# Opening stage of a gated cross-attention kernel: keys and values of its tiles in two PSUM banks by turns, other slots for the latents and weights

## The reference, cut to what matters

```python
lat = layer_norm(layernorm(x), ln_lat_g, ln_lat_b)      # x: (4, 512, 256)
ctx = layer_norm(ctx_1024, ln_ctx_g, ln_ctx_b)          # (4, 1024, 256)
q = (lat @ Wq)                                          # 16 heads of 64
k, v = split(ctx @ Wkv, 2)
k = apply_rope(k, cos, sin)                             # k*cos + swapped halves*(-sin, sin)
attn = softmax(clip(q @ k.T / 8, -11, 11)) @ v
x = x + tanh(g_xattn) * (attn @ Wo + bo)
x = x + tanh(g_ffn) * moe_ffn(layernorm(x))             # 4 experts, top 2, exact gelu
```

## Time and profile before

| | |
|---|---|
| time of three runs, median (lowest to highest) | 1143.57 us (1140.17 to 1144.3) |
| the profiled execution: its own time | 1138.58 us |
| its span (first to last instruction) | 1137.0 us |
| mean granted TensorE clock | 0.985 of full |
| TensorE busy | 1078.4 us, 95% of the span |
| VectorE / ScalarE / GpSimd busy | 951.9 / 653.4 / 536.8 us |
| the stage ahead of the attention, up to the first scores | 46.62 us |

### The profile page before, as it was taken

One profiled execution on the slowest core, in us unless ns is written; L12 is line 12 of the kernel. 1 busy time (PEld: TensorE's weight loads), 2 busy tenths in 40 slices (PEclk: granted clock), 3 DMA queues, 4 the chain that ended last, 5 costly groups with the idle time before them and its releaser, 6 DMA issues.

```text
span 1137.0 us, 22328 instructions
## 1 busy us (share of the span) xinstructions
PE 1078.4 (95%) x7949; PEld 718.2 (63%) x7949; DVE 951.9 (84%) x1772; ACT 653.4 (57%) x1259; POOL 536.8 (47%) x551
## 2 busy tenths in 40 slices
PE   5799999999999999999999999999999998899995
PEld 4455555656565555556555555655445998899994
DVE  6698899898989989898999989879976757777675
ACT  4555557655555765454566655544556666577662
POOL 6433376333427634342654334417641655656661
PEclk9999999999999999999999999989999999899998
DMA  6100000000000000000000000601264342565344
GB/s 167 52 10 11 19 25 24 15 12 13 10 20 21 28 11 11 19 11 20 19 29 10 11 10 10 201 1 39 71 202 141 120 141 85 171 193 181 113 143 146
DMA packets 59188, 72.04 MB, mean 63 GB/s; under 512 B 11580, under 2 KB 52168, under 8 KB 59081
## 3 DMA queue, kind: packets, MB, share of 16 engines
q1 hardware_dynamic: 54840, 61.30, 17.5%
q0 software_dynamic: 3360, 8.53, 2.0%
q10 hardware_dynamic: 880, 0.79, 0.2%
HBM read 54.84 MB, written 16.54 MB: 63 GB/s over the span
## 4 chain that ended last, share of the span: by engine, by line
PE 74%; DVE 13%; issue 4%; POOL 3%; ACT 2%; DMA 2%; SPq 0%; DVEq 0%; POOLq 0%
PE pv L1808 17%; PE sc L1794 14%; PE kv L1739 5%; PE kv L1741 5%; PE kv L1740 5%; PE sc L1739 4%; PE sc L1740 4%; PE sc L1741 4%; PE tr L1780 3%; PE mi L1739 2%; PE mi L1818 2%; PE mi L1740 2%; PE mi L1741 2%; DVE acc L1167 2%; DVE prob L1152 2%
## 5 line engine op out<-in xcount | busy, mean ns | idle before, releaser
L926 ACT ACTIVATE prob<-sc 128x1024 f32<-128x1024 f32 x256 | 249.4, 1029 | 203.4 <-PE sc L1794 200.8
L711 POOL TENSOR_TENSOR rot_s<-k_raw,sinb 128x256 f32<-128x256 f32 x128 | 110.8, 866 | 383.9 <-ACT k_raw L871 383.8
L1808 PE MATMUL pv<-prob,val 128*32 128x512 f32 x2048 | 247.9, 602 | 3.0 <-DVE recip L1186 3.0
L1152 DVE TENSOR_SCALAR prob<-prob 128x1024 f32<-128x1024 f32 x256 | 181.3, 721 | 48.1 <-ACT prob L926 47.0
L1794 PE MATMUL sc<-q_hid,w2all 64*128 64x512 f32 x1536 | 214.1, 411 | 0.0
L1794 PEld LDWEIGHTS sc<-q_hid,w2all 64*128 64x128 f32 x1536 | 135.7, 186 | 100.4 <-issue 56.2
L1167 DVE TENSOR_TENSOR acc<-acc,prob 128x1024 f32<-128x1024 f32 x120 | 178.2, 1505 | 0.0
L715 POOL TENSOR_TENSOR rot_c<-rot_c,rot_s 128x256 f32<-128x256 f32 x128 | 111.8, 874 | 41.6 <-DVE rot_c L1141 27.0
L1808 PEld LDWEIGHTS pv<-prob,val 128*32 128x32 f32 x2048 | 56.9, 110 | 113.4 <-issue 92.1
L1739 PE MATMUL kv<-w2all,acts 128*128 128x512 f32 x256 | 115.2, 450 | 6.6 <-DVE rot_c L1141 5.3
L1741 PE MATMUL kv<-w2all,acts 128*128 128x512 f32 x256 | 103.5, 404 | 0.0
(11 more groups left out here) (306 smaller groups left out, 2372.8 us busy)
## 6 DMA issues: line engine op xcount, KB each, us to landing
prob<-in_L_ffn_w SPq DMA_DIRECT2D x17, 1024.0 KB, 5.4
slots_x<-lat_r SPq DMA_DIRECT2D x1, 5016.0 KB, 18.7
rows<-slots_x SPq DMA_DIRECT2D x19, 264.0 KB, 5.0
rows<-in_ctx SPq DMA_DIRECT2D x32, 128.0 KB, 2.1
w_raw<-in_L_xattn_Wq SPq DMA_DIRECT2D x16, 256.0 KB, 2.8
w_raw<-in_L_xattn_Wo SPq DMA_DIRECT2D x64, 64.0 KB
acc<-in_L_ffn_w SPq DMA_DIRECT2D x16, 256.0 KB, 5.1
acc<-in_L_ffn_w SPq DMA_DIRECT2D x5, 512.0 KB, 5.2
```

The lines of the kernel that those rows point to most:

```text
L711: g.tensor_tensor(rot_s[:].rearrange("p (h a c) -> p h a c", h=4, a=2), kh[:, :, ::-1, :], sinb[:, t].unsqueeze(1).to_broadcast([P, 4, 2, ...
L926: a.activation(prob[:, s % 2, i, :], sc[i][:], ACT.Exp, scale=DH ** -0.5).then_inc(exp_done[i], 1)
L1152: v.tensor_scalar(prob[:, s % 2, i, :], prob[:, s % 2, i, :], EXP_LOW, EXP_HIGH, ALU.max, ALU.min).then_inc(clamped[i], 1)
L1808: last = mm(pv[g * 32:(g + 1) * 32, :], val[:, u % 2, 2 * c + i, at:at + 32], prob[:, s % 2, i, h * N:(h + 1) * N], start=c == 0 and i == ...
```

## The change

The `before()` lists get another order on four engines, and two of the waits change:

- `kv_bank`: in the first unit the tiles with an odd number have their keys and values in the bank `pv`, which nothing else uses before the attention's second step. `kv_make` of tile i then waits for `rot_cos` of tile i-2 and not i-1. `kv_evac` and `rot_cos` read the bank in question. In all other units everything stays in `kv`.
- `kv_evac` waits for `rot2` (the first of GpSimd's two instructions of `rotate`) and no longer for `rot`; in exchange GpSimd itself waits for its own last `rot` ahead of the product. This holds for all units.
- VectorE: `lat_stats` stands in slot 3 (was 2), `lat_norm` in slot 5 (was 4, behind the rotation), `q_low` in slot 9 (was 8), all of them and `wkv_low` now ahead of `rot_cos` and `k_low` of their slot; `wkv_low` of units 1 to 3 in slots 6, 8, 10 (was 4, 6, 8).
- ScalarE: `wq_round` in slot 3 (was 4), `q_round` in slot 8 (was 7), `wkv_round` in slots 3, 4, 7 (was 3, 5, 7).
- GpSimd: `lat_scale` and `wq_low` ahead of `rotate` in their slots, `lat_scale` in slot 4 (was 3).
- TensorE: `ctx_turn` ahead of `k_turn`; `q_make` in slot 8 (was 7).

```diff
+        def kv_bank(b, u, t):
+
+            return pv if is_first(b, u) and t % 2 else kv
+
...
@@ rotate
                 pool.wait_ge(kraw_out, n + 1)
+                wait(pool, rot, n)
                 g.tensor_tensor(rot_s[:].rearrange("p (h a c) -> p h a c", h=4, a=2), kh[:, :, ::-1, :],
...
@@ gpsimd, before
-                    if 0 <= t - 3 < ST:
-                        rotate(0, 0, t - 3)
-                    if t == 3:
+                    if t == 4:
                         lat_scale(0)
                     if t == 5:
                         wq_low(0, 0)
+                    if 0 <= t - 3 < ST:
+                        rotate(0, 0, t - 3)
...
@@ kv_evac
-                wait(act, rot, kv_no(b, u, t))
-                a.activation(k_raw[:], kv[:, 0:UW], ACT.Copy).then_inc(kraw_out, 1)
-                a.activation(val[:, u % 2, t, :], kv[:, UW:2 * UW], ACT.Copy).then_inc(kv_out, 1)
+                wait(act, rot2, kv_no(b, u, t))
+                bank = kv_bank(b, u, t)
+                a.activation(k_raw[:], bank[:, 0:UW], ACT.Copy).then_inc(kraw_out, 1)
+                a.activation(val[:, u % 2, t, :], bank[:, UW:2 * UW], ACT.Copy).then_inc(kv_out, 1)
...
@@ scalar, before
-                    if t == 4:
+                    if t == 3:
                         wq_round(0, 0)
                     if t in (5, 6):
                         lat_affine(0, t - 5, sc[1][:, (t - 5) * N:(t - 4) * N])
-                    if t == 7:
+                    if t == 8:
                         q_round(0, 0)
-                    if t in (3, 5, 7):
-                        wkv_round(t // 2)
+                    if t in (3, 4, 7):
+                        wkv_round((3, 4, 7).index(t) + 1)
...
@@ vector, before
-                    if t == 2:
-                        wkv_low(0)
+                    if t in (2, 6, 8, 10):
+                        wkv_low((2, 6, 8, 10).index(t))
                     if 0 <= t - 2 < ST:
                         ctx_split(t - 2)
...
                         dve.wait_ge(const, 6)
+                    if t == 3:
                         for i in range(NT):
                             lat_stats(0, i)
                             dve.wait_ge(l_st, i + 1)
                             lat_aggregate(0, i)
+                    if t == 5:
+                        for i in range(NT):
+                            lat_norm(0, i)
+                    if t in (6, 7):
+                        lat_low(0, t - 6)
+                    if t == 9:
+                        q_low(0, 0)
                     if 0 <= t - 3 < ST:
                         rot_cos(0, 0, t - 3)
                     if 0 <= t - 4 < ST - 1:
                         k_low(0, 0, t - 4)
-                    if t == 4:
-                        for i in range(NT):
-                            lat_norm(0, i)
-                    if t in (6, 7):
-                        lat_low(0, t - 6)
-                    if t == 8:
-                        q_low(0, 0)
-                    if t in (4, 6, 8):
-                        wkv_low((t - 2) // 2)
...
@@ kv_make
-                wait(pe, rot1, kv_no(b, u, t))
+                wait(pe, rot1, t - 1 if is_first(b, u) else kv_no(b, u, t))
...
@@ tensor, before
                         kv_make(0, 0, t - 3)
+                    if 0 <= t - 1 < ST:
+
+                        wait(pe, c_affd, t - 2)
+                        ctx_turn(0, t - 1, sc[0][:, ((t - 1) % 2) * N:((t - 1) % 2 + 1) * N])
                     if 0 <= t - 4 < ST - 1:
                         k_turn(0, 0, t - 4)
-                    if 0 <= t - 1 < ST:
-
-                        wait(pe, c_affd, t - 2)
-                        ctx_turn(0, t - 1, sc[0][:, ((t - 1) % 2) * N:((t - 1) % 2 + 1) * N])
                     if t in (5, 6):
                         lat_turn(0, t - 5, sc[1][:, (t - 5) * N:(t - 4) * N])
-                    if t == 7:
+                    if t == 8:
                         q_make(0, 0)
```

More of the change, by code:

```diff
@@ L1140, in rot_cos @@
                 dve.wait_ge(kv_out, kv_no(b, u, t) + 1)
-                v.tensor_tensor(rot_c[:].rearrange("p (h c) -> p h c", h=8), kv[:, 0:UW].rearrange("p (h c) -> p h c", h=8),
+                v.tensor_tensor(rot_c[:].rearrange("p (h c) -> p h c", h=8),
+                                kv_bank(b, u, t)[:, 0:UW].rearrange("p (h c) -> p h c", h=8),
                                 cosb[:, t].unsqueeze(1).to_broadcast([P, 8, HALF]),
@@ L1767, in kv_make @@
                 pe.wait_ge(c_ready, tile_no(b, t) + 1)
-                wait(pe, rot1, kv_no(b, u, t))
+                wait(pe, rot1, t - 1 if is_first(b, u) else kv_no(b, u, t))
                 for k in range(KT):
-                    last = three(kv[:].rearrange("p (w n) -> p w n", w=2), lambda l: ctx_t[:, l, k, t * P:(t + 1) * P],
+                    last = three(kv_bank(b, u, t)[:].rearrange("p (w n) -> p w n", w=2), lambda l: ctx_t[:, l, k, t * P:(t + 1) * P],
                                  lambda l: wkv[:, l, k, :].rearrange("p (w n) -> p w n", w=2)[:, :, u * UW:(u + 1) * UW],
@@ L1905, in before @@
                         kv_make(0, 0, t - 3)
-                    if 0 <= t - 4 < ST - 1:
-                        k_turn(0, 0, t - 4)
                     if 0 <= t - 1 < ST:
@@ L1911, in before @@
                         ctx_turn(0, t - 1, sc[0][:, ((t - 1) % 2) * N:((t - 1) % 2 + 1) * N])
+                    if 0 <= t - 4 < ST - 1:
+                        k_turn(0, 0, t - 4)
                     if t in (5, 6):
                         lat_turn(0, t - 5, sc[1][:, (t - 5) * N:(t - 4) * N])
-                    if t == 7:
+                    if t == 8:
                         q_make(0, 0)
```

## The result

| | before | changed |
|---|---|---|
| median (lowest to highest) of 7 runs each | 1142.26 us (1140.17 to 1144.3) | 1133.73 us (1129.95 to 1135.23) |
| profiled execution, its span | 1138.58, 1137.0 us | 1131.16, 1129.6 us |
| first scores | 46.62 us | 39.01 us |
| third step's scores | 57.51 us | 49.58 us |
| span behind the first scores | 1090.4 us | 1090.6 us |

A forecast was written before the change was run, and what follows sets the result against it. No engine is full before the first scores; their start decides. 18.9 + 18.4 + 0.8 + 1.6 = 39.7 against 46.62 gives 6.9, less 0.5 for the clock 6.4, from the median 1143.57: 1137.0 us, range 1133 to 1142.

The forecast's parts named there:

- Part 1: VectorE, slots 2 and 3: latents' statistics behind tile 3 cover the 1.11 us wait for x; tile 0's rot_cos at 13.3.
- Part 2: GpSimd's latent chain decides when VectorE gets its next work: lat_norm can start at 18.9 us, where it was 19.52.
- Part 3: VectorE from lat_norm to the last wkv_low has no idle time: 18.4 us of work plus 0.8 of new waits.
- These two are the bank's and `k_raw`'s: VectorE's waits of 1.17 and 2.63 us for a tile's values, counted as removed by the two banks: 3.8 us.
- The rival that "the turn of the banks doesn't free anything": Both value waits come back under another name, only Parts 1 and 2 gain, 1 to 2.5 us: 1141.5 us; chance 0.12.
- The new list's own waits: VectorE after lat_norm: tile 7's split waits for ScalarE, which waits for tile 6's split; with small ones 0.8 us.
- Part 4: VectorE and GpSimd slowing each other in the stage: some 3.4 us of old overlaps held in 18.4, plus 1.6 new.
- The rival that pays each in full: All ten or so overlaps block VectorE for a whole add, 7.4 us: gain 4.6, 1139.0 us; chance 0.25.
- Part 5: TensorE's lower clock from kv_make of tile 6 on, no longer hidden by VectorE: 0.5 us (0 to 1.3) off the gain.

The follow-up runs named there:

- narrow_rotation: The changed kernel with GpSimd's product and add of the first unit's keys over 2 of every 32 columns, the rest unrotated; ratio to before 0.9890, first scores 34.75 us.
- banks_raw_only: The kernel before, old order of all lists, with the two banks and the early release of the raw keys; ratio to before 1.0014, first scores 47.15 us.
- q_later_only: The kernel before with only the first query a slot later (q_make and q_round in 8, q_low in 9); ratio to before 0.9978, first scores 43.85 us.
- before_busy_pe: The kernel before with five unused matmuls of 512 columns on TensorE ahead of tile 7's kv_make; ratio to before 0.9976, first scores 45.57 us.
- late_pairs_raw_late: The changed kernel with the last two wkv_low pairs in the attention's first step and raw keys released by GpSimd's add; ratio to before 0.9906, first scores 36.71 us.

## Why the prediction was right or wrong

- **Part 1** was right: 1.1 us forecast, 1.3 measured by taking it back.
- **Part 2** was right: `lat_norm` at 19.13, forecast 18.9.
- **Part 3 has the step that failed.** "These two are the bank's and `k_raw`'s": they were not. The buffers alone left both waits (0.92 and 3.91) and lost 0.5 us; the order alone took 6.7 of the 7.6 us. Of the 1.17 some 0.8 was a `wkv_round` ahead of ScalarE's copy, by its rows. The 2.63 was in the main the query in TensorE's queue, and the query's place alone brought the first scores forward by 2.8 us. The banks are worth 0.8 to 1.1 us, and only with the query out of the way. That the sum came out near is luck: the new order removes the same two waits for another reason, and the banks then take away two that the order alone has at other tiles (1.31 and 0.55). The rival that "the turn of the banks doesn't free anything" was right on the banks and wrong on its time, 1141.5, because it gave the waits to them too. Work without overlaps and waits was forecast at 18.4 - 3.4 = 15.0 us, and is 15.1 (15.63 less waits of 0.50). The new list's own waits were forecast at 0.8 and measured at 0.43.
- **Part 4** was mis-sized, and in the old share more than in the new. Old overlaps 3.4 plus 1.6 new made 5.0 us; `narrow_rotation` measures 4.2. The 3.4 held 1.1 of the CAST that met `wq_low` (1.38 for 0.29), and this overlap is gone in the new list. Without it the old ones are 2.3 by the rows, and 1.9 are new. They are where they were expected, at the pairs, the norms and the CASTs. The rival that pays each in full (7.4) falls. The Trainium skill's rule on the shared ports (SBUF — State Buffer, "Who interferes with whom") agrees with single rows: the CAST at 32.16 ended 0.14 us after GpSimd's product (31.67 to 32.84), and with GpSimd's instructions cut short CASTs take 0.29 again.
- **Part 5** was mis-sized: 0.5 us taken off, nothing measured, since tiles 6 and 7 of the new stage run at the higher level (mean granted clock 1.00 from 33.55 to 37.0). The old stage, on the other hand, had paid 1.05 us at its end, which the comparison of the two starts took in by itself.
- **The 3.3 us between 1137.0 and 1133.73**: 0.5 from the clock, 0.7 from the list of VectorE (38.96 for 39.7), 1.3 because the median of before is 1142.26 in seven runs and was 1143.57 in three, and 0.8 left, which is the medians' difference (8.5) less what the profiles show (7.6 to 7.9), inside the interval.
- `kv_evac`'s wait for `rot2` costs and gains nothing, as costed. The slots of the pairs were taken as part of the new overlaps, and are worth nothing either.

Open: how the 6.7 us of the order divide over all its moves. The rows say in which stretch they lie (0.5, 1.6 and 4.6 us), not to which move each belongs. Two were measured alone, the query on the old list (2.8, with the clock's 1.2 in it) and the statistics on the new (1.3). `wkv_round`'s share is read from rows and was not tried.

## What to carry to other kernels

A wait is named by what came last, here ScalarE's copy, and a buffer close by makes an easy culprit. Before giving the wait to it, read the queue rows of each engine in the chain over that very stretch: a row without a wait that stands behind unrelated work says that the order is the cause. Look first at what stands behind the last item of the list at the end of a stage; here that was 4.6 of 7.6 us. When one engine's list ends a stage, take out of it what nobody reads until later; and expect two good moves to undo each other once another engine is the bound.

## What the runs showed of the hardware that was not expected

- Matmuls of 512 columns had a pitch of 0.43 us (25.79, 26.21, 26.64 of the kernel before) while the column of the granted clock read 1.00 for 25.0 to 26.6, and 0.23 us with the same reading later (36.65 to 36.88). From 34 us on the column and the pitch agree (0.50 and 0.43 in `banks_raw_only`). In the first 27 us the level is better read from the pitch.
- The lower level can come and go with small shifts of the order. The six matmuls behind the turn of context tile 6 took 1.49 us in the kernel before, 2.73 in `banks_raw_only` and 2.70 in `q_later_only`; TensorE's idle time ahead of that turn had been 1.65, 2.26 and 1.64 us, so the length of this one pause doesn't tell them apart. Five matmuls put in a pause elsewhere (`before_busy_pe`) kept the higher level for the six behind it.
- With the code behind the stage unchanged or nearly so, the span behind the first scores was between 1086.7 us (`late_pairs_raw_late`, 1123.4 less 36.71) and 1096.3 us (`q_later_only`, 1140.1 less 43.85) in single profiles. A single profile's span says nothing of an edit of a few us here; the starts within the stage repeat better: `lat_norm` came between 18.95 and 19.34 in the eight kernels that have the same VectorE list up to it, and between 19.52 and 20.10 in the five with the old list, each 8.9 us after its wait for x had ended.
